# VectorE adds an output between the next step's maxima and its transposes, and two query projections follow the weighted sum

## The reference

```
for each of 16 heads (head size 128):
    k, q, v = xn W_K^T, xn W_Q^T, xn W_V^T          # 2048 x 128 each
    p = softmax(causal(q k^T) / sqrt(128))           # 2048 x 2048, lower triangle
    attention += (p v) W_O_head^T                    # 2048 x 256
ffn = hadamard(silu(xn W1^T) * (xn W3^T)) W2^T       # hidden size 1024
```

## Time and profile before

| | before |
|---|---|
| median of 3 runs | 1471.53 us (1470.75 to 1471.66) |
| the profiled execution | 1468.4 us, span 1466.5 us |
| granted TensorE clock, mean | 0.983 |
| TensorE busy (matmuls) | 1350.7 us, 92% |
| TensorE weight loads | 1189.0 us, 81% |
| VectorE busy | 1048.4 us, 71% |
| ScalarE busy | 836.4 us, 57% |
| GpSimd busy | 838.5 us, 57% |
| DMA | 335.13 MB, the main queue's packets 73.1% of 16 engines' span |

### The profile page before, as it was taken

One profiled execution on the slowest core, in us unless ns is written; L12 is line 12 of the kernel. 1 busy time (PEld: TensorE's weight loads), 2 busy tenths in 40 slices (PEclk: granted clock), 3 DMA queues, 4 the chain that ended last, 5 costly groups with the idle time before them and its releaser, 6 DMA issues.

```text
span 1466.5 us, 26458 instructions
## 1 busy us (share of the span) xinstructions
PE 1350.7 (92%) x8104; PEld 1189.0 (81%) x8104; DVE 1048.4 (71%) x2389; ACT 836.4 (57%) x1623; POOL 838.5 (57%) x532
## 2 busy tenths in 40 slices
PE   3999999969999999999999999999999999999986
PEld 2878888758888888888888888888888888888875
DVE  6643300378888888888888888888888888888882
ACT  3322244366666666666666666666666666666662
POOL 4410000065757585858585857576767676767574
PEclk7899999989999999999999999999999999999998
DMA  4100056589897978888888887978898888888885
GB/s 145 68 1 0 0 151 194 157 249 284 256 284 250 283 244 282 246 284 260 276 254 281 248 286 253 283 252 284 251 281 247 281 262 264 271 261 271 263 266 167
DMA packets 278458, 335.13 MB, mean 229 GB/s; under 512 B 62736, under 2 KB 251280, under 8 KB 273808
## 3 DMA queue, kind: packets, MB, share of 16 engines
q1 hardware_dynamic: 278416, 334.65, 73.1%
HBM read 173.08 MB, written 161.48 MB: 228 GB/s over the span
## 4 chain that ended last, share of the span: by engine, by line
PE 27%; issue 26%; POOL 24%; DVE 8%; ACT 6%; DMA 4%; SPq 4%; POOLq 1%; DVEq 0%; ACTq 0%
POOL pt_lo L371 21%; PE ps L811 9%; PE ps L812 9%; PE ps L813 9%; SPq L275 3%; DMA scratch<-raw 3%; ACT raw L529 3%; DVE had L723 3%; ACT pt_hi L538 1%; POOL v_lo L376 1%; DVE raw L733 1%; POOL wqk_lo L355 1%; DMA raw<-w3t 1%; DVE acc L749 1%; POOL wqk_hi L353 1%
## 5 line engine op out<-in xcount | busy, mean ns | idle before, releaser
L371 POOL TENSOR_TENSOR pt_lo<-pt_lo,pt_hi 128x640 fp32r<-128x640 f32 (+11 forms) x384 | 662.0, 1756 | 241.7 <-ACT pt_hi L538 241.7
L529 ACT ACTIVATE raw<-ps,had 128x1024 f32<-128x1024 f32 (+7 forms) x384 | 329.2, 865 | 323.0 <-DVE had L726 263.3
L733 DVE STREAM_TRANSPOSE raw<-raw 128x2048 f32<-128x2048 f32 (+15 forms) x256 | 322.0, 1292 | 94.5 <-ACT raw L529 92.3
L811 PE MATMUL ps<-pt_hi,v_hi 128*128 128x256 f32 (+1 forms) x1152 | 324.6, 282 | 20.7 <-POOL pt_lo L371 19.1
L812 PE MATMUL ps<-pt_lo,v_hi 128*128 128x256 f32 (+1 forms) x1152 | 329.6, 286 | 0.0
L813 PE MATMUL ps<-pt_hi,v_lo 128*128 128x256 f32 (+1 forms) x1152 | 327.5, 284 | 0.0
L538 ACT CAST pt_hi<-pt_lo 128x640 fp32r<-128x640 f32 (+11 forms) x384 | 282.3, 812 | 12.0 <-DMA pt_lo<-scratch 11.9
L811 PE MATMUL ps<-k_hi,q_hi 128*128 128x512 f32 (+3 forms) x640 | 238.2, 372 | 18.5 <-ACT raw L529 18.4
L723 DVE TENSOR_REDUCE had<-ps 128x1 f32<-128x1024 f32 (+1 forms) x256 | 237.9, 950 | 8.1 <-PE ps L813 8.1
L811 PEld LDWEIGHTS ps<-pt_hi,v_hi 128*128 128x128 f32 x1152 | 219.8, 191 | 29.6 <-issue 21.8
L813 PE MATMUL ps<-k_hi,q_lo 128*128 128x512 f32 (+3 forms) x640 | 233.9, 365 | 0.0
(11 more groups left out here) (101 smaller groups left out, 2202.8 us busy)
## 6 DMA issues: line engine op xcount, KB each, us to landing
all_values<-raw SPq DMA_DIRECT2D x16, 1024.0 KB, 5.0
v_next<-all_values SPq DMA_DIRECT2D x16, 1024.0 KB, 5.4
scratch<-raw SPq DMA_DIRECT2D x64, 256.0 KB, 5.4
pt_lo<-scratch SPq DMA_DIRECT2D x16, 1024.0 KB, 5.5
scratch<-raw SPq DMA_DIRECT2D x64, 240.0 KB, 5.2
pt_lo<-scratch SPq DMA_DIRECT2D x16, 960.0 KB, 6.1
scratch<-raw SPq DMA_DIRECT2D x64, 224.0 KB, 5.4
pt_lo<-scratch SPq DMA_DIRECT2D x16, 896.0 KB, 5.0
```

The source lines that it names most:

```text
L371: pool.tensor_tensor(lo, lo.bitcast(F32), hi.bitcast(F32), ALU.subtract).then_inc(pt_lo_done, 1)
L529: act.activation(to[:, first // P:(first + n) // P], ps[:, a * BANK:a * BANK + n].rearrange("p (i g k) -> p i g k", g=4, k=BLK), ACT.Exp, ...
L733: dve.transpose(v, v).then_inc(blocked, 1)
L811: pe.matmul(dst, a[0], b[0], start=start, stop=False, skip_group_check=True)
```

## The change

Two edits, and no operation on data is added or removed.

On VectorE the addition of an output (L749) stood in each step behind `z_to_lo` and ahead of the two `maxima`. It now stands behind them: in steps 0, 2, 4 and 6 behind the maxima and the reciprocals, in steps 1, 3 and 5 behind the maxima and the step's second `z_to_lo`, and in step 7 behind the maxima and ahead of the low part of K0. The transposes come after it in all steps.

On TensorE the projection Q1 in step 0 and Q0 in step 6 stood ahead of the weighted sum of the step. They now stand behind it. Q2 in step 1 and Q3 in step 5 already did. K0 in step 7 stays right behind the scores.

```
--- before.py
+++ after.py
@@ -767,21 +767,23 @@
                 for s in range(6 if over else STEPS):
                     if s in O_SMALL and not absent(O_SMALL[s][0]):
                         z_to_lo(h + O_SMALL[s][0], O_SMALL[s][1])
-
-                    back, z = (O_SMALL if s % 2 else O_BIG)[(s - 1) % STEPS]
-                    if s == 0:
-                        back -= 1
-                    if not absent(back):
-                        output(h + back, z)
                     if not over:
                         maxima(h, s, 0)
                         maxima(h, s, 1)
                     if s % 2 == 0 and not (first and s == 0) and not (over and s > 0):
                         reciprocals(*((h, s // 2 - 1) if s else (h - 1, 3)))
+
+                    back, z = (O_SMALL if s % 2 else O_BIG)[(s - 1) % STEPS]
+                    if s == 0:
+                        back -= 1
+                    if s == 7:
+                        output(h + back, z)
                     if s == 7 and more:
                         kq_to_lo(h, ("K", 0))
                     if s in O_BIG and not absent(O_BIG[s][0]):
                         z_to_lo(h + O_BIG[s][0], O_BIG[s][1])
+                    if s != 7 and not absent(back):
+                        output(h + back, z)
                     if not over:
                         transpose_blocks(h, s, 0)
                     if s == 7 and more:
@@ -1005,12 +1007,12 @@
                         project_kq(h, ("K", 0))
                     if s in O_SMALL and not absent(O_SMALL[s][0]):
                         output(h + O_SMALL[s][0], O_SMALL[s][1])
+                    if not absent(Z_BIG[s][0]):
+                        weighted_sum(h + Z_BIG[s][0], Z_BIG[s][1], s % 2)
                     if s == 0 and not over:
                         project_kq(h, ("Q", 1))
                     if s == 6 and more:
                         project_kq(h, ("Q", 0))
-                    if not absent(Z_BIG[s][0]):
-                        weighted_sum(h + Z_BIG[s][0], Z_BIG[s][1], s % 2)
                     if s == 1 and not over:
                         project_kq(h, ("Q", 2))
                     if s == 3 and more and not over:
```

More of the change, by code:

```diff
@@ L769, in period @@
                         z_to_lo(h + O_SMALL[s][0], O_SMALL[s][1])
[L771 to L775, removed]
                     if not over:
```

## The result

The changed kernel takes 1550.29 us (median of 4 runs, 1541.92 to 1551.8) against 1471.14 us before: ratio 1.0527, 95% interval 1.0489 to 1.0565. The prediction of 1511 us had the direction, and missed half of the size: it forecast 40 us more than before, and 79 came.

The account below looks back on a forecast made before the run. TensorE's in-order queue was taken to bound the kernel, with 3.45 us of stops per head. 2.75 us per head over 15 heads, less the last head's gain, gave +40 us: median about 1511 us, range 1500 to 1524.

Parts of the forecast that it names:

- the walk: Step-by-step replay of one head, each engine starting when its last releaser is done; gave a middle head of about 75.0 us.
- K0's start: Step 7, main term: K0 waits 2.56 us for VectorE's addition, 5.6 us behind the first score; 2.66 us with restart.
- Q2's wait: Step 1: Q2 waits 1.9 us for the addition of z3; TensorE leaves the step about 1.25 us later.
- the cover of TensorE's edit in step 0: Step 0: Q1 moves behind the 2.5 us sum, so TensorE does not stop for the later addition of z2.
- the old stops in steps 3 and 4: TensorE's stops of 0.68, 1.45 and 0.86 us were to shrink to nothing or little.
- The clock falls: Rival, 5%: TensorE's clock drops to 1.2 GHz for about 3.5 us behind the new stop; 26 us more, 1537 us.
- the sum: Adding up: 0.1 + 2.66 = 2.75 us per head with a K0, 15 heads, 41 us; together +40 us.
- a gain of 1 us: Last head, which has neither Q0 nor K0: keeps about 1 us of the gain.
- The output z6 kept its stop: Step 3: the 1.45 us stop at the output z6 was to be gone.
- GpSimd's hold in front of step 6's sum: Step 6: with Q0 behind the sum, TensorE waits some 0.5 us there for GpSimd's low part of p.
- SyncE's queue carries on the lateness: Rival, 12%: step 1's 1.25 us lateness stays in SyncE's queue; 1.1 us more per head, 1527 us.
- the upstream gain: Scores of step 5 start about 1.1 us earlier, all lost again by step 6; rival that it survives 10%, 1497 to 1503 us.

Follow-up runs that it names:

- e4: Changed kernel, both waits kept, but TensorE fills them with 14 matmuls ahead of Q2 and 19 ahead of K0 whose results are overwritten: 1514.1 us.
- e6: Kernel before with TensorE's edit alone (Q1 and Q0 behind the sums), VectorE as before: 1491.7 us.
- e8: e3 with the addition of z5 and the low part of z6 between the two maxima of step 3: 1467.6 us.
- e12: e8 with the addition of z7 in step 5 ahead of the maxima too: 1468.1 us.
- e1: Changed kernel with the addition of z1 in step 7 back ahead of the maxima: 1499.9 us.
- e3: Changed kernel with the additions of z1 (step 7) and z3 (step 1) both back ahead of the maxima: 1469.1 us.
- e2: Changed kernel with the addition of z3 in step 1 back ahead of the maxima: 1516.5 us.
- e10: Changed kernel with 14 filling matmuls ahead of Q2 only, K0's wait left bare: 1521.8 us.
- e13: e10 with 5 more matmuls of 256 columns ahead of K1, making the head longer: 1534.0 us.
- e15: e10 with 15 more matmuls of 256 columns ahead of K1, making the head longer: 1559.3 us.

## Why the prediction was wrong

**The direction and the walk were right.** K0's start 5.6 us behind the first score (5.65 measured), its idle time and releaser, Q2's wait (1.9 us between the end of the sum and Q2; 680.82 less some 679.0), the cover of TensorE's edit in step 0: each is in the trace. Of the old stops in steps 3 and 4, the first is gone and the others shrink only in part. The walk's head of 75.0 us is what e4 runs at with the clock held, and e4's 1514.1 us stands beside the predicted 1511.

**The step that failed** is the one that I called "The clock falls" and gave 5%: "The new stop is 2.6 us, shorter than both, so I hold the full clock for likely". The row that I leaned on is true: a stop of 3.28 us with the full clock behind it. The reading was wrong. I took the stop's length for what decides, and one row of one head as proof; in the changed kernel the clock fell in 14 heads of 14 at the 2.41 us of K0, and in 10 of 14 at the 1.70 us of Q2, a stop for which I had not asked the question at all. So the sum had the falls at nothing, and they cost some 37 us.

That one row does not even repeat. In the changed kernel the same stop of head 0, ahead of both new waits, has a fall behind it:

```profile
295.24 0.50 PE L813 MATMUL ps<-k_hi,q_hi 128*128 128x512 f32 x1 [3.27 <-ACT raw L529]
297.00:298.00 1.00, 1.00 (x3) 0.76 (x3) 1.00 (x1) 0.62 (x2) 0.29 (x1) 0.50 0.23 33
```

Twelve of the traces of this case have this stop, at 3.27 to 3.31 us, and eleven of them have a fall at it or right behind it; the one with the full clock is that of the kernel before. And the trace before held a row against the reading. TensorE went idle at 299.0 us there, in front of the longer stop of the earlier trace rows; this is the clock 2 us later, with TensorE still idle:

```profile
300.00:301.00 1.00, 0.00 (x0) 0.00 (x0) 1.00 (x2) 0.00 (x0) 0.92 (x2) 1.00 0.99 410
301.00:302.00 1.00, 0.00 (x0) 0.00 (x0) 1.00 (x4) 0.00 (x0) 0.89 (x1) 0.51 0.93 372
```

There the clock was down 2 us into a stop, and the stop that I forecast was 2.56 us long.

The section of the Trainium skill that I cited against the change ("TensorE: Matmul & The Clock Gate", section "HAM oscillation — how this bites in real kernels") gave the better direction, but its example has longer waits than the 2.41 us here. It did not say that a stop of this size is enough, and the prediction should not have written that by that rule the result would be the rival's.

The price of a fall came out near by luck. The earlier trace rows show the lower clock from the restart at 303.49 to about 307.8 us, so 4.3 us and not the 3.5 that I read, which would have priced a fall at 2.2 us; the falls of the middle heads last 3.4 us, take 1.7 us from TensorE and add 1.4 us to a head behind K0. And there were two stops per head to count, not one, so that the rival's 26 us were some 37.

**Smaller terms.** They offset each other in part, which is luck. A head without a fall takes 2.6 us more than before (74.9 against 72.3), not 2.75, so 2 us less over the fourteen heads. Outside of them, in head 0 and from head 15 on, the changed kernel's execution is 9 us longer than the one before, where the sum had 2; in the last head I had even forecast a gain of 1 us, and from its first score to the end it takes 4.7 us more. No run takes that apart. The output z6 kept its stop (1.27 us), of which I had written that it would be gone: the addition of z5 took the place of the low part as its releaser. A stop of 0.49 us at the output z0, released by the addition of z7, was not in the walk at all. GpSimd's hold in front of step 6's sum was put at 0.5 us; the output z1 of 645.13 and the sum at 646.06 leave about 0.2 us. That SyncE's queue carries on the lateness (12%) is not needed: e4 has both waits, and its head is the walk's. That GpSimd uses up the upstream gain fits e6, e8 and e12, in which TensorE stops for its low part.

## What to carry to other kernels

An instruction that frees a buffer belongs ahead of whatever waits for the engine that needs the buffer. Before moving one back, list who waits for its semaphore: here those of z1, z3, z5 and z7 had a TensorE instruction close behind, and two of them cost all. A new stop on TensorE costs up to its length and perhaps a fall of the clock, and here the falls were about as dear as the stops (some 37 of 79 us); a stop that had no fall once, in one head, proves nothing, so count that cost once for each new stop and keep it in the range. A wait can be kept cheap for the clock by matmuls that lead to nothing, but taking the wait out is worth more (1469 against 1514 us).

## What the runs showed of the hardware that I had not expected

The clock fell behind stops of 1.70 us (e1: 9 falls, with no longer stop in those heads), while stops of 1.55 us in the same kernel's sister e3 had none in the heads where they recur. The same 2.41 us stop had a fall in 14 heads of 14 in the changed kernel, in 9 of 14 in e2 and in 3 of 14 in e10, and in e13 to e15 the number rose to 10 with the matmuls that made the head longer. In 11 of 12 traces the clock fell at head 0's stop of 3.3 us, in 5 of these before TensorE had restarted. The spread of the changed kernel's runs (1541.92 to 1551.8, 0.6%) is larger than that of before (0.1%), as it would be if the number of falls differed between runs; the fastest of the four runs also has the highest mean clock, 0.960 against 0.954 to 0.956. Only one execution has its clock in full, so this last point is argued.
